# The fused attention and routing stage with every lagged phase one step nearer to the attention

## The reference, cut to what matters

```python
qkv = layernorm(x) @ w_qkv.T
q_phi, k_phi = sorf_phi(rope(q)), sorf_phi(rope(k))     # exp of 128 projections a head
S, sum_k = einsum("chlm,chld->chmd", k_phi, v), sum(k_phi, axis=2)
numer = einsum("chlm,chmd->chld", q_phi, S)
denom = maximum(einsum("chlm,chm->chl", q_phi, sum_k), 1e-6)
x = x + layernorm((numer / denom[..., None]) @ w_out.T)
...
scores = sigmoid(layernorm(x) @ gate_w.T)
_, idx = top_k(scores + bias, 4)
# each (token, choice) gets the next free place of its expert, up to 512
...
x = x + layernorm(experts + shared_expert)
```

## Time and profile before

| what | value |
|---|---|
| median of 3 runs | 2308.94 us (2304.46 to 2310.68) |
| the profiled execution | 2301.66 us, its span 2299.8 us |
| PE busy | 1851.5 us, 81% of the span |
| DVE, ACT, POOL busy | 1254.8, 1123.4, 783.1 us |
| PE's mean granted clock | 0.925 of full speed |
| DMA | 402.00 MB, 175 GB/s |
| fused stage | from about 905 us to 1530 us of the span |

### The profile page before, as it was taken

One profiled execution on the slowest core, in us unless ns is written; L12 is line 12 of the kernel. 1 busy time (PEld: TensorE's weight loads), 2 busy tenths in 40 slices (PEclk: granted clock), 3 DMA queues, 4 the chain that ended last, 5 costly groups with the idle time before them and its releaser, 6 DMA issues. The chain is left out here.

```text
span 2299.8 us, 33677 instructions
## 1 busy us (share of the span) xinstructions
PE 1851.5 (81%) x12976; PEld 889.3 (39%) x12976; DVE 1254.8 (55%) x2226; ACT 1123.4 (49%) x1369; POOL 783.1 (34%) x715
## 2 busy tenths in 40 slices
PE   3999999999979998897888885208999999377665
PEld 3444444444438784232222222104444444133221
DVE  5567676766630001588888888703444444255465
ACT  2545454555526665676776674304444454123232
POOL 0000000000000000127777677765878888300000
PEclk9999999999989999999999998659999999788787
DMA  5353534446258885777876754325799988666765
GB/s 178 101 193 119 172 129 161 137 154 198 89 160 202 208 213 126 185 209 185 222 202 191 217 173 132 129 57 111 155 202 210 221 200 189 120 255 217 255 212 203
DMA packets 215407, 402.00 MB, mean 175 GB/s; under 512 B 29652, under 2 KB 108884, under 8 KB 198624
## 3 DMA queue, kind: packets, MB, share of 16 engines
q1 hardware_dynamic: 110800, 221.36, 33.9%
q10 hardware_dynamic: 67584, 122.17, 15.4%
q0 software_dynamic: 36864, 56.32, 12.7%
HBM read 236.54 MB, written 174.46 MB: 179 GB/s over the span
## 5 line engine op out<-in xcount | busy, mean ns | idle before, releaser
L315 PE MATMUL s_proj<-s_xT,keep_wqkv 128*128 128x512 f16 x1536 | 341.8, 379 | 0.0
L1192 POOL DMA_INDIRECT slot_dram<-s_filled,s_slots x256 | 291.0, 1137 | 83.1 <-issue 79.1
L1278 POOL DMA_INDIRECT acc_dram<-s_y,s_slot x128 | 201.3, 1573 | 75.1 <-issue 35.7
L834 PE MATMUL s_y<-keep_wo,s_at_hl 128*128 128x512 f16 x768 | 186.7, 395 | 40.2 <-ACT s_z L925 39.0
L315 PEld LDWEIGHTS s_proj<-s_xT,keep_wqkv 128*128 128x128 f16 x1536 | 147.8, 98 | 183.2 <-issue 12.6
L294 PE MATMUL s_proj<-keep_wqkv,s_xT 128*128 128x512 f16 x768 | 179.0, 391 | 32.7 <-ACT s_xT L462 32.7
L358 POOL TENSOR_SCALAR s_rstd<-s_mv 128x4 f32<-128x4 f32 x16 | 16.0, 998 | 519.1 <-DVE s_mv L373 519.1
L406 DVE TENSOR_TENSOR s_by_cos<-s_proj,s_table 128x1024 f32<-128x1024 f32 x64 | 78.4, 1224 | 186.7 <-PE s_proj L315 186.5
L478 ACT ACTIVATE s_hl<-s_rot 128x1024 f16<-128x1024 f32 x64 | 67.6, 1057 | 224.9 <-DVE s_rot L419 224.9
L611 ACT ACTIVATE s_phi<-s_logits 128x1024 f32<-128x1024 f32 x128 | 131.1, 1024 | 85.3 <-PE s_logits L632 85.3
L904 ACT ACTIVATE s_phi<-s_logits 128x1024 f32<-128x1024 f32 x128 | 131.2, 1025 | 76.3 <-PE s_logits L803 75.6
(11 more groups left out here) (156 smaller groups left out, 3317.0 us busy)
## 6 DMA issues: line engine op xcount, KB each, us to landing
s_x<-x_in SPq DMA_DIRECT2D x32, 1024.0 KB, 8.3
qk_dram<-s_hl ACTq DMA_DIRECT2D x32, 1024.0 KB, 5.9
keep_ahead<-qk_dram SPq DMA_DIRECT2D x48, 512.0 KB
s_w<-W_in SPq DMA_DIRECT2D x96, 256.0 KB, 3.6
acc_dram<-s_zero SPq DMA_DIRECT2D x17, 1024.0 KB, 11.1
v_dram<-s_v ACTq DMA_DIRECT2D x16, 1056.0 KB, 5.7
s_v<-v_dram SPq DMA_DIRECT2D x16, 1056.0 KB, 11.0
s_spread<-share_dram SPq DMA_DIRECT2D x64, 256.0 KB
```

The source lines that it names most:

```text
L315: mm = nc.tensor.matmul(out[:, 512 * b:512 * b + 512], left, right, start=(c == 0 and i == 0), stop=(c == EC - 1 and i == 2))
L834: mm = nc.tensor.matmul(y[m % 2][:], at_hl[n % 2][:, s, c, a * P:(a + 1) * P], keep["wo"][:, w, c, :], start=(c == 0 and i == 0), stop=(c ...
L1192: nc.gpsimd.indirect_dma_start(out=io["slot"], out_offset=bass.IndirectOffsetOnAxis(ap=slots[n % 2][:, a * K + j:a * K + j + 1], axis=0), ...
L1278: nc.gpsimd.indirect_dma_start(out=io["acc"], out_offset=bass.IndirectOffsetOnAxis(ap=slot[e % RING][:, a, 0:1], axis=0), in_=y[e % 2][:, ...
```

## The change

The two lines of lags become smaller by one, save that `fill` comes nearer by two: it stood two steps behind the count, in the step of the first scatters, and now stands one step behind the count. The product with the reciprocals (`divide`) and `make_at_high` move from step 4n+6 to 4n+5, the step right behind `make_share`, and `make_at_low` from 4n+7 to 4n+6. `make_share` itself stays in step 4n+4. The attention keeps its place. The last step of the stage is 83 instead of 84. The loops, the buffers, the waits and what each instruction does are the same; the order of SP's and of POOL's instructions among themselves does not change.

```diff
-        PROJECT, MEASURE, SCALE, ADD, SPLIT, TURN, COPY, GATE = 8, 9, 10, 11, 12, 13, 14, 14
-        SCORE, CHOOSE, PLACE, WEIGH, FILL, SEND = 18, 18, 19, 19, 21, 21
+        PROJECT, MEASURE, SCALE, ADD, SPLIT, TURN, COPY, GATE = 7, 8, 9, 10, 11, 12, 13, 13
+        SCORE, CHOOSE, PLACE, WEIGH, FILL, SEND = 17, 17, 18, 18, 19, 20
...
-                n = group_at(s, A + 2)
+                n = group_at(s, A + 1)
                 if n is not None:
                     make_at_high(n)
...
-                n = group_at(s, A + 2)
+                n = group_at(s, A + 1)
                 if n is not None:
                     divide(n)
-                n = group_at(s, A + 3)
+                n = group_at(s, A + 2)
                 if n is not None:
                     make_at_low(n)
```

## The result

| | before | after |
|---|---|---|
| median of 4 runs | 2307.03 us (2304.46 to 2310.68) | 2374.72 us (2371.95 to 2376.22) |
| ratio, with its 95% interval | | 1.0291 (1.0272 to 1.031) |
| the profiled execution | 2301.66 us, span 2299.8 | 2374.29 us, span 2372.5 |
| from the first to the fifth reading of the denominators (groups 0 to 4) | 104.05 us | 120.18 us |
| from the fifth to the sixteenth (groups 4 to 15) | 374.56 us | 434.59 us |

The change made the kernel slower by 67.7 us between the medians, and by 72.7 between the two spans. The three rows that cut the stage show where it is: 16.1 us more in the early groups, 60.0 in the eleven periods of the steady part (39.5 us a period, from 34.1), 2.0 less at the end. That is 74.1 us; the spans differ by 1.4 less, which lies outside these rows. The rows come from one profile of each kernel.

The account below looks back on a forecast made before the run. The prediction took the chain over DVE, ACT and PE that `divide` starts in kind 2 as the bound. Steady groups 58.8, early groups 15.6, end -6 gave +68.4 us: forecast 2374 us, range 2338 to 2415.

Parts of the forecast that it names:

- `divide` meets an unfinished `spread` and DVE stands.: Kind 1, steady groups: DVE reaches `divide` at 1162.47, `spread` lands at 1165.07, so it waits 2.6 us with nothing else changed.
- The store ahead of `share`.: End of kind 0: `store_rows`, issued 0.27 us ahead, makes `share` 2.4 us late; likeliest case, 47 in 100.
- the first rival: The store does not delay `share`: wait 2.6 us, or 3.3; 2335 to 2350 us; 26 in 100.
- The floor of 2.6 us: Lower bound of DVE's wait before `divide` in kind 1, if the store delays nothing.
- The sign that was named for it: SP's queue: the wait for `share` grows from 1.2 to over 3 us; 1.2 would mean no store effect.
- The wait of 5.0 us.: DVE before `divide` in kind 1, steady groups: `spread` lands at 1167.5; bounds 2.6 and 7.6 us.
- The saving of 0.4 us.: Each steady period: `fill` waits less for POOL and `make_share` loses the copy ahead of it; ends 0 and 0.8 us.
- The clock.: PE behind its longer idle time runs at half clock, mostly beside `choose`; 0.3 us a group, ends 0 and 1.5.
- The sum.: Whole stage: 4.9 us in each of twelve steady groups, early groups 15.6, end 6 saved: +68.4 us.
- Faster, since the wait never comes: Rival: `spread` is back when DVE reaches `divide` in kind 1; 10.8 us saved, 2291 to 2298 us; 3 in 100.
- Store and spread hinder each other: Rival, steady groups: wait 7.6 us and 1.2 for the clock, +110 us, 2412 to 2419 us; 20 in 100.
- The steps take the wait up: Rival: light kinds 2 and 3 give back what kind 1 loses; nothing changes but the end; 4 in 100.

Follow-up runs that it names:

- the divide alone: Kernel before, all lags as before, with only `divide` and `make_at_high` moved to step 4n+5 and `make_at_low` to 4n+6: 2330.33 us.
- `choose` first: Changed kernel with `choose` ahead of `divide` on DVE and `make_score` ahead of `make_at_high` on ACT: 2342.84 us.
- the store put back: Changed kernel with only `store_rows` one step later, where it stood before the change: 2336.51 us.
- the wait covered: Last run: changed kernel with `choose` ahead of `divide`, `make_at_high` one step later behind the second `phi`, `make_at_low` behind `weigh`: 2291.75 us.
- kernel before with a store put there: Kernel before with `store_turned` (1 MB) two steps later, just ahead of the small writes of `share`: 2304.63 us.
- two stores ahead: Changed kernel with `store_x1` (1 MB) two steps later, to be issued just ahead of `store_rows`: 2398.78 us.

## Why the prediction was right, and where its sizes were off

The time (2374 forecast), the sign and the mechanism came out. Point by point:

- **`divide` meets an unfinished `spread` and DVE stands.** Right, in 16 of 16 groups. Without the store the changed kernel loses 31 us, with it 37 more. (The run with the divide alone lost 25, with the gain of the exponential in it, so it is no part of this sum.)
- **The store ahead of `share`.** Right in kind, and it is the likeliest case, not the first rival: taking it away took the wait from about 6 to 2.8 us. The delay was larger than the 2.4 us of the prediction: 5.32 - 2.40 = 2.9 us. The term that was short is the store's end: by its own terms 1155.86 + 0.9 + 2.8 = 1159.6, some 3.5 us after the first small write; measured, packets of the store still began to move after 1358, over 3.6 us after that write at 1354.42, and `spread` was issued 1359.74. The floor of 2.6 us for the wait without a store was good: 2.5 to 3.3 measured. The sign that was named for it failed: SP's wait for `share` was to grow from 1.2 to over 3 us and came to 2.2, since 1.4 us of the delay show as longer issue (2.63 us for 1.27), which no row of before has.
- **The wait of 5.0 us.** Too small by one: 5.98 in the period shown, 6.25 in the mean of groups 4 to 15. To the 0.5 us of the later `share` comes the landing, 1359.74 to 1366.77, 7.03 us and not the 6.54 of the earlier trace rows.
- **The saving of 0.4 us.** Too small: `fill` in kind 3 saved 0.62 (6.19 for 6.81) and the copy that left kind 0 0.20 (7.81 for 8.01), 0.82 in all, just past the upper end that I gave.
- **The clock.** I added 0.3 us a group; nothing of it is seen. The slower matmuls lay beside `choose`. In the run with `choose` first they did not, and there the clock is part of the period of 36.9 us.
- **The sum.** 5.98 - 0.82 = 5.16 us in the period shown, where I had 4.9, so a period of 39.0 there and 39.5 in the mean, for 38 to 39; eleven periods took 60.0 us more, where I had 53.9. The early groups cost 16.1 (forecast 15.6), but not as they were split: 4.2, 6.7, 3.4 and 1.8 us from group to group, where 3.45, 5.5 and a mean between floor and that stood; the sum is met by luck. The end saved 2.0 with the wait of group 15 in it, where 4.9 - 6 = -1.1 was forecast. The profile gives 72.7 in the span for the 68.4 of the sum, the medians 67.7. That the forecast of 2374 met the median so closely is in part luck: a wait that was 1 us too small a group stood beside a saving that was 0.4 too small and a clock term that was 0.3 too large, and the start of the sum was taken in the middle between one execution and the median.
- **The rivals.** "The store delays nothing" (2335 to 2350 us) is what the kernel with the store put back shows, 2336.51. "Faster, since the wait never comes" needed a covered wait, and with the wait covered the kernel is faster by 10 us. That this is close to the 10.8 us of the rival is no test of its sum: the end saved 8.8 us where it had 6, and the early groups cost 4.6 where it had nothing. "Store and spread hinder each other" needed a wait of 7.6 us in all groups and had 2412 to 2419 us; the wait was 6.25, and only its smaller part, a landing 0.5 us later, is of that kind. "The steps take the wait up" is out: the light steps gave back nothing of it.

Of the two rules that I weighed from the Trainium skill (DMA: Bandwidth & Descriptors, section Queues, rings and completion order), the turns between queues would let the small writes pass, with a wait nearer 3.3 us by the prediction. The wait was 6, and 24 of their 32 packets moved only at the store's end; 8 passed beside 503 of the store, so the trace shows at most weak turns. That a semaphore lands only after the earlier writes of its DMA engine would give the same kind of delay; here most data packets themselves moved late, so the rows can't show whether this rule adds to it. Nor do they show whether the late packets stood in the DMA engines' queues or had not yet been handed to them; that the store's end sets the time is what is shown.

## What to carry to other kernels

Before a phase is moved nearer to its producer, look at what covers the round trip between them, here a write, a wait and a read of 1 MB, and count what each engine has queued behind the instruction that will wait: an in-order queue turns one wait into a stop of all three engines. A shift of whole schedules also moves transfers, and a large store that is issued just ahead of a small write on the critical path delays it: here by 2.9 us, for 1 MB that moved in 3, while the same store did not delay it when it was issued 1.5 us behind the write. The order of programs doesn't say which comes first; the issue times in the trace do. Once the wait is there, work that needs nothing of it belongs ahead of it, on each engine in its queue and not on the waiting one alone.

## What the runs showed of the hardware that was not expected

- Four writes of 8 KB take SP 1.27 us to issue, and 2.63 us when ACT has issued a store of 1 MB 0.15 us ahead (kernel after) or 0.24 us ahead (kernel before with a store put there), so it is not a matter of the schedule. Where the store came 0.66 us behind the start of the writes they took 1.27 us still, but `spread` was issued 3.56 us after the first and not 2.40 (group 6 of the last run).
- `spread`, 1.05 MB read with each row spread over 32 partitions, moves at 0.2 MB in a microsecond (1.06 MB in 5 us), a plain store of the same size at over 0.3 (1.03 MB in 3 us, in the rows above), and SP's queue itself 0.31 in the stretch just behind, where the load of x follows (0.62 MB in 2 us). The moving of `spread` is thus some 5 of the 8.9 us between the first write of `share` and the landing that the prediction worked out for the kernel before. That the spreading is what makes it slow is likely and was not tested.
- In group 5 `share` or `spread` is late in seven of the eleven kernels: DVE waits 9.52 us there with the divide alone, and 5.33 in the kernel before with a store ahead, where no other group but the first waited. In the kernel after and with two stores ahead the group doesn't stand out, and in the two runs with `choose` first DVE comes too late to show it. What is in the way stays open. With the divide alone the period from group 5 to 6 takes 40.7 us where its neighbours take 34.6 and 34.1, so some 6 of that kernel's 24.9 us are this one wait; in the other kernels it is less.
